# Gram products ahead of the QKV maximum pass, joined row sums in the softmax stage, and no cleared maxima, in a quantised decoder layer

## The reference

```python
def _pot_scale(x):                       # one scale for the whole tensor
    m = jnp.maximum(jnp.max(jnp.abs(x)), 1e-08)
    return jnp.exp2(jnp.ceil(jnp.log2(m / INT8_MAX)))
...
h = (x - mu) * jax.lax.rsqrt(var + LN_EPS)
h = h * fq_round(ln_gamma) + fq_round(ln_beta)
qkv = fq_floor(fq_floor(h) @ fq_round(w_qkv))
...
dots = jnp.einsum('bhnd,bhmd->bhnm', q, k) * temp
dots = fq_floor(dots)
attn = jax.nn.softmax(dots, axis=-1)
attn = fq_floor(attn)
out = jnp.einsum('bhnm,bhmd->bhnd', attn, v)
out = fq_floor(fq_floor(out) @ fq_round(w_out))
...
# cross-attention, with k and v from ctx
kv = jnp.einsum('bthd,bthe->bhde', k, v)
att = jnp.einsum('bqhd,bhde->bqhe', q, kv) * scale
```

## Time and profile before

| what | us |
|---|---|
| median of three runs | 481.63 (481.36 to 481.78) |
| the profiled execution | 479.8 |
| its span | 478.0 |
| QKV maximum pass, 28.84 to 73.34 | 44.50 |
| softmax stage, 183.73 to 317.08 | 133.35 |
| DVE busy over the span | 420.0 |
| ACT busy | 350.2 |
| PE busy | 233.2 |
| POOL busy | 149.9 |

### The profile page before, as it was taken

One profiled execution on the slowest core, in us unless ns is written; L12 is line 12 of the kernel. 1 busy time (PEld: TensorE's weight loads), 2 busy tenths in 40 slices (PEclk: granted clock), 3 DMA queues, 4 the chain that ended last, 5 costly groups with the idle time before them and its releaser, 6 DMA issues.

```text
span 478.0 us, 6808 instructions
## 1 busy us (share of the span) xinstructions
PE 233.2 (49%) x1541; PEld 106.5 (22%) x1541; DVE 420.0 (88%) x1396; ACT 350.2 (73%) x789; POOL 149.9 (31%) x323
## 2 busy tenths in 40 slices
PE   0269973878677733122222222119997718116031
PEld 0228411323122210011001111003342616102031
DVE  5879897889899999999999999958986985977967
ACT  3678983879899955999999999954776745537133
POOL 2500002001000002888889888870000005520010
PEclk9969995999755555555555555558999775557557
DMA  7500000000344520788888888792001300000002
GB/s 268 145 0 2 0 0 2 22 22 24 132 176 176 191 95 23 163 187 187 187 197 188 182 188 187 165 211 46 2 2 44 106 1 1 0 1 0 0 0 89
DMA packets 84210, 43.16 MB, mean 90 GB/s; under 512 B 69064, under 2 KB 74456, under 8 KB 84059
## 3 DMA queue, kind: packets, MB, share of 16 engines
q1 hardware_dynamic: 82618, 42.69, 34.2%
q10 hardware_dynamic: 1568, 0.21, 0.3%
HBM read 7.75 MB, written 1.58 MB: 20 GB/s over the span
## 4 chain that ended last, share of the span: by engine, by line
DVE 53%; PE 21%; issue 16%; ACT 7%; DMA 1%; DVEq 1%; ACTq 0%
PE ps L475 20%; DVE mem L1308 12%; DVE mem L1055 6%; DVE mem L1213 4%; DVE d_max L1058 4%; DVE mem L1496 2%; DVE row_max L1308 2%; DVE m L1633 2%; DVE m L1634 2%; ACT mem L903 2%; ACT mem L933 1%; DVE r_now L1054 1%; DMA bkv<-in_L_xattn_bv 1%; DVE row_code L1054 1%; DVE neg_max L1054 1%
## 5 line engine op out<-in xcount | busy, mean ns | idle before, releaser
L475 PE MATMUL ps<-mem 64*128 64x256 bf16 (+5 forms) x1188 | 175.0, 355 | 131.7 <-DMA mem<-mem 87.4
L933 ACT ACTIVATE mem<-mem,neg_max 128x256 f32<-128x256 int16 x256 | 126.2, 494 | 13.2 <-DVE neg_max L1054 9.4
L475 PEld LDWEIGHTS ps<-mem 64*128 64x128 bf16 (+3 forms) x1188 | 72.2, 122 | 229.0 <-issue 126.7
L1308 DVE CUSTOM_DVE_ANT_0 mem<-ps,fold,c 128x256 int16<-128x256 f32 x256 | 111.3, 471 | 0.0
L433 POOL TENSOR_SCALAR mem<-mem,r_now 128x256 int16<-128x256 f32 x176 | 80.9, 478 | 80.9 <-DVE r_now L1054 80.8
L1213 DVE TENSOR_TENSOR mem<-mem 128x1024 bf16<-128x1024 bf16 x82 | 54.3, 688 | 6.2 <-ACT mem L873 4.0
L888 ACT ACTIVATE mem<-ps,c 128x1024 bf16<-128x1024 f32 x48 | 48.4, 1294 | 1.6 <-PE ps L475 1.6
L933 ACT ACTIVATION_READ_ACCUMULATOR mem<-mem,neg_max 128x1 f32 x256 | 47.7, 186 | 0.0
L903 ACT ACTIVATE mem<-ps,c 128x1024 int16<-128x1024 f32 x32 | 36.4, 1211 | 13.8 <-DVEq L1250 8.5
L433 POOL TENSOR_SCALAR bv_fine<-mem,r_now 128x256 int16<-128x256 f32 x80 | 36.8, 479 | 5.0 <-DVE r_now L1054 5.0
L1058 DVE TENSOR_REDUCE d_max<-ps 128x1 f32<-128x1024 f32 (+1 forms) x34 | 38.0, 1126 | 0.3 <-PE ps L475 0.3
(11 more groups left out here) (207 smaller groups left out, 380.4 us busy)
## 6 DMA issues: line engine op xcount, KB each, us to landing
mem<-mem SPq DMA_DIRECT2D x64, 256.0 KB, 2.4
mem<-in_L_attn_w_qkv SPq DMA_DIRECT2D x1, 1536.0 KB, 9.3
mem<-in_x SPq DMA_DIRECT2D x2, 512.0 KB, 5.0
mem<-in_x SPq DMA_DIRECT2D x1, 1024.0 KB, 5.5
out<-mem SPq DMA_DIRECT2D x4, 256.0 KB, 2.2
xattn_matrix<-mem SPq DMA_DIRECT2D x1, 512.0 KB
mem<-in_L_attn_w_out SPq DMA_DIRECT2D x1, 512.0 KB, 5.0
mem<-in_L_ffn_W SPq DMA_DIRECT2D x2, 256.0 KB, 4.6
```

Source lines behind the costliest of these rows:

```text
L475: return te.matmul(o_, l_, r_, start=start, stop=stop)
L933: ins = sc.activation(e_ring[:, u % 4, pos], y_ring[:, u % 4, pos], ACT.Exp, scale=scale_reg, bias=neg_max[:, u % 4, pos:pos + 1], accum_o ...
L1308: ins = ve.tensor_tensor_reduce(y_ring[:, slot, pos], ps[:, 2 * slot + pos // 2, (pos % 2) * N:(pos % 2 + 1) * N], shift, col("g_dots"), - ...
```

## The change

- The eight Gram matrices are made in PE's queue ahead of the QKV maximum pass, four before the `across` of the weights and h and four behind it, in banks 4 to 6. ACT evicts them before and among its three w_qkv codes and at n = 1, and PE waits for two evictions before unit 2. The sums of ctx move to n = 12 and `a1` to one batch after each of n = 15 to 18 and 24 to 27. The 16 small bias activations of ACT's front are split: 8 stay, 4 come before the Gram evictions, 4 at n = 6.
- POOL's two clearings of `run_max` are gone. In both maximum passes ACT writes its first three units straight into `run_max`, and DVE starts to fold at the fourth.
- `temperature()` stands behind the semaphore that releases the first codes of the code pass.
- In the softmax stage `row_code` is float32, rounded by adding and subtracting 1.5 x 2^23. All row sums stay in `row_sums`, 128 x 256. There is one reciprocal and one `r_now` to a group, over eight rows, and no `sum_run`; one minimum over `row_sums` ends the stage. The index of `row_sums` is computed in ACT's loop for each piece. DVE's loop is written out for all 32 groups, and the order in a group is another.
- SP issues the transpose of group grp - 2 behind the copy of group grp + 4.

```diff
+WHOLE = 1.5 * 2.0 ** 23
...
-        sum_run = sb("sum_run", [P, 2, 4])
-        row_code = sb("row_code", [P, 2, 8], I16)
+        row_code = sb("row_code", [P, 2, 8])
-        row_inv = sb("row_inv", [P, 4, 4])
+        row_inv = sb("row_inv", [P, 2, 8])
-        row_sum = sb("row_sum", [P, 4, 4])
+        row_sums = sb("row_sums", [P, B * GROUPS * 8])
...
-            for grp in range(B * GROUPS - 2):
+            for grp in range(B * GROUPS):
                 if grp + STAGES < B * GROUPS:
                     stage_group("codes", grp + STAGES, grp % STAGES)
-                transpose_group(grp)
+                if grp >= 2:
+                    transpose_group(grp - 2)
...
-            pool.wait_ge(sem("gb_codes"), 1)
-            pl.memset(run_max, 0.0).then_inc(sem("run_max_zero"), 1)
-
-
-            pool.wait_ge(sem("qkv_scale"), 1)
-            pl.memset(run_max, 0.0).then_inc(sem("run_max_zero"), 1)
-
...
-            across(7, diag6[:, 2:4], 2)
-
-            def gram_half(b, part):
-                bank, pos = (6, 7, 6)[b // 3], b % 3
-                for k in range(2 * part, 2 * part + 2):
+
+            def gram_of(b):
+                bank, pos = 4 + b // 3, b % 3
+                for k in range(4):
                     last = mm(ps[:, bank, pos * (D + 1):(pos + 1) * (D + 1)], ctx_sb[:, 4 * b + k, 0:D],
                               ctx_sb[:, 4 * b + k], k == 0, k == 3)
-                if part == 1 and b in (2, 5, 7):
+                if b in (2, 5, 7):
                     last.then_inc(sem("gram_ps"), 1)
+
+            pe.wait_ge(sem("ctx_ones"), 1)
+            pe.wait_ge(sem("ctx_loaded"), 16)
+            for b in range(4):
+                gram_of(b)
+            pe.wait_ge(sem("xw_T"), 1)
+            across(7, diag6[:, 2:4], 2)
+            for b in range(4, B):
+                gram_of(b)
...
-            def a1_main(half):
-                for b in range(4 * half, 4 * half + 4):
-                    mm(ps[:, 6 + half, (b % 4) * P:(b % 4 + 1) * P], gram[:, b, 0:D], xw_T[:, 1], b % 4 == 0, False)
+            def a1_main(half, b):
+                mm(ps[:, 6 + half, b * P:(b + 1) * P], gram[:, 4 * half + b, 0:D], xw_T[:, 1], b == 0, False)
...
-                if n == 6:
-                    pe.wait_ge(sem("ctx_loaded"), 16)
-                    pe.wait_ge(sem("ctx_ones"), 1)
-                    pe.wait_ge(sem("xw_T"), 1)
                 if n == 12:
                     pe.wait_ge(sem("wh_scale"), 1)
-                if n == 18:
-                    pe.wait_ge(sem("gram_ready"), 1)
-                if 6 <= n < 22:
-                    gram_half((n - 6) // 2, n % 2)
-                if n == 27:
                     pe.wait_ge(sem("gram_ready"), 3)
-                    pe.wait_ge(sem("bias_rows"), 1)
+                    pe.wait_ge(sem("bias_rows"), 3)
                     sums_of_ctx()
-                if n == 28:
-                    a1_main(0)
-                if n == 31:
+                if n in (15, 16, 17, 18):
+                    a1_main(0, n - 15)
+                if n == 21:
                     pe.wait_ge(sem("cs_r2"), 1)
                     a1_bias(0)
-                if n == 32:
-                    a1_main(1)
-                if n == 34:
+                if n in (24, 25, 26, 27):
+                    a1_main(1, n - 24)
+                if n == 30:
                     a1_bias(1)
...
+            bias_rows(4, 6)
+            gram_eviction(0)
             act.wait_ge(sem("wh_scale"), 1)
             for k in range(3):
+                if k == 2:
+                    gram_eviction(1)
...
+                if n == 1:
+                    gram_eviction(2)
+                if n == 6:
+                    bias_rows(6, 8)
+                if n == 14:
...
-                        sc.activation(abs_t[:, nth % 3], ps[:, s:s + 2].rearrange("p a n -> p (a n)"),
+                        sc.activation(run_max[:, nth] if nth < 3 else abs_t[:, nth % 3],
+                                      ps[:, s:s + 2].rearrange("p a n -> p (a n)"),
...
-                                            accum_out=row_sum[:, u % 4, pos:pos + 1])
+                                            accum_out=row_sums[:, bass.ds(unit * 4 + pos, 1)])
...
-            temperature()
...
             dve.sem_inc(sem("cast_a"), 4)
+            temperature()
...
-            def fold_sums(grp, half):
+            def row_reciprocal(grp, half):
 
                 dve.wait_ge(sem("exp_done"), 2 * grp + 6)
-                dve.wait_ge(sem("sum_folded"), grp + 1)
-                ve.tensor_tensor(sum_run[:], sum_run[:], row_sum[:, 2 * half:2 * half + 2], ALU.min)\
-                    .then_inc(sem("sum_folded"), 1)
-
-            def row_reciprocal(unit, k):
-
-                dve.wait_ge(sem("exp_done"), unit + 5)
-                ve.reciprocal(row_inv[:, k], row_sum[:, k]).then_inc(sem("row_inv"), 1)
-
-            def row_scale(unit, k):
-
-                dve.wait_ge(sem("row_inv"), unit + 1)
-                ts(r_now[:, k], row_inv[:, k], FINE, None, ALU.mult).then_inc(sem("row_scale"), 1)
+                ve.reciprocal(row_inv[:, half], row_sums[:, 8 * grp:8 * grp + 8]).then_inc(sem("row_inv"), 1)
+
+            def row_scale(grp, half):
+
+                dve.wait_ge(sem("row_inv"), grp + 1)
+                ts(r_now[:, 2 * half:2 * half + 2].rearrange("p u h -> p (u h)"), row_inv[:, half], FINE, None,
+                   ALU.mult).then_inc(sem("row_scale"), 2)
 
             def step(grp, half, new, old):
 
-                other = 2 * (1 - half)
-                if old:
-                    row_reciprocal(2 * grp - 2, other)
                 dve.wait_ge(sem("y_ready_u"), 2 * grp + 6)
                 if new:
                     dve.wait_ge(sem("dots_codes_unit"), 2 * grp + 4 + 2 * STAGES)
-                ts(row_code[:, half], row_max[:, half], 1.0, None, ALU.mult).then_inc(sem("row_code"), 1)
+                ts(row_code[:, half], row_max[:, half], WHOLE, -WHOLE, ALU.add, ALU.add).then_inc(sem("row_code"), 1)
                 if new:
-
+                    if old:
+                        dve.wait_ge(sem("exp_done"), 2 * grp + 3)
                     codes(2 * grp + 2, 1 - half, 0, (0,))
                 dve.wait_ge(sem("row_code"), grp + 1)
                 ts(neg_max[:, 2 * half:2 * half + 2].rearrange("p u h -> p (u h)"), row_code[:, half],
                    col("ns_dots"), None, ALU.mult).then_inc(sem("neg_max"), 1)
-                if old:
-                    row_scale(2 * grp - 2, other)
                 if new:
                     codes(2 * grp + 2, 1 - half, 0, (1, 2, 3))
                 if old:
-                    row_reciprocal(2 * grp - 1, other + 1)
+                    row_reciprocal(grp - 1, 1 - half)
                 if new:
-
-                    codes(2 * grp + 3, 1 - half, 1, (0, 1))
+                    codes(2 * grp + 3, 1 - half, 1, (0,))
                 if old:
-                    row_scale(2 * grp - 1, other + 1)
-                    fold_sums(grp - 1, 1 - half)
+                    row_scale(grp - 1, 1 - half)
                 if new:
-                    codes(2 * grp + 3, 1 - half, 1, (2, 3))
+                    codes(2 * grp + 3, 1 - half, 1, (1, 2, 3))
 
             groups = B * GROUPS
-            ve.memset(sum_run[:], 3.0e38).then_inc(sem("sum_folded"), 1)
             dve.wait_ge(sem("dots_codes_unit"), 2 + 2 * STAGES)
             for k in range(2):
                 codes(k, 0, k, (0, 1, 2, 3))
             step(0, 0, True, False)
-            with dve.Fori(0, groups // 2 - 1) as i:
-                for k in range(2):
-                    step(i * 2 + 1 + k, 1 - k, True, True)
+            for grp in range(1, groups - 1):
+                step(grp, grp % 2, True, True)
             step(groups - 1, 1, False, True)
-            for k in range(2):
-                row_reciprocal(2 * groups - 2 + k, 2 + k)
-            for k in range(2):
-                row_scale(2 * groups - 2 + k, 2 + k)
-            fold_sums(groups - 1, 1)
-
-
-            dve.wait_ge(sem("sum_folded"), groups + 1)
-            link(ve.tensor_reduce(col("m"), sum_run[:].rearrange("p u h -> p (u h)"), AX.X, ALU.min))
+            row_reciprocal(groups - 1, 1)
+            row_scale(groups - 1, 1)
+
+
+            dve.wait_ge(sem("exp_done"), B * DOT_UNITS + 4)
+            link(ve.tensor_reduce(col("m"), row_sums[:], AX.X, ALU.min))
```

More of the change, by code:

```diff
@@ L821, in _, with bias_rows @@
             act.wait_ge(sem("bkv_loaded"), 32)
-            for b in range(B):
-                sc.activation(bv_sel[:, b], bkv[:, 1], ACT.Copy, scale=ident[0:B, b:b + 1])
-                ins = sc.activation(bk_sel[:, b], bkv[:, 0], ACT.Copy, scale=ident[0:B, b:b + 1])
-            ins.then_inc(sem("bias_rows"), 1)
+            def bias_rows(first, end):
+                for b in range(first, end):
+                    sc.activation(bv_sel[:, b], bkv[:, 1], ACT.Copy, scale=ident[0:B, b:b + 1])
```

(11 more changed lines are left out.)

25 lines of the change are left out of this document (12 added, 13 removed).

## The result

The changed kernel took 468.72 us (median of four runs, 468.06 to 470.23) against 481.50 (four runs, 479.68 to 481.78) before: a ratio of 0.975, 95% interval 0.971 to 0.978. The forecast was 470.1, with a range of 465 to 477. The profiled execution took 468.85 us, with a span of 467.1 against 478.0.

What follows compares the result with a forecast made beforehand. DVE was taken to bound the softmax stage, with engines waiting in turn in the QKV maximum pass. Terms -3.8 - 1.3 - 6.3 - 0.1 = -11.5 us brought the median 481.63 to 470.1, range 465 to 477.

Steps and rivals of the forecast that it cites:

- What bounds the kernel now: Softmax stage: DVE sets the 4.18 us group, ACT close behind; QKV maximum pass: no engine fills it, engines wait in turn.
- The start, -0.8: Front: without POOL's clearing the across and first units come earlier despite Gram products on PE; -0.8 us, nothing to -1.3.
- two of its signs: Front, in the new trace: the across near 23.7 us and unit 0 at 28.1 us.
- Rival 2, the clock: Front and QKV pass: the Gram move gives nothing if PE's matmuls run at half clock; 473.9 us, chance 0.12.
- The pace, -3.0: QKV maximum pass: moving Gram work out shortens eleven d_max intervals by 3.0 us, between 1.8 and 5.2.
- The first units written to `run_max`, 0: Both maximum passes: DVE's three saved folds lie behind ACT or are made up at the pass's end; zero.
- `temperature()`, -1.3: Start of the code pass: seven small DVE instructions of 0.19 us go behind the release; -1.3 us, lower bound -0.6.
- The softmax stage, -6.3: Fewer DVE instructions bring a group to 3.97 us over 32 groups; -6.3 us, bounds -7.4 and 0.
- The three floors: Softmax group: ACT needs 3.94 us, POOL 3.90, and DVE 3.94 with one wait for POOL.
- Rival 1, POOL's lock: Softmax stage: two of three small DVE operations wait for POOL, gain 0.6 instead of 6.3 us; 475.8 us, chance 0.20.
- Rival 3, the register instruction: Softmax stage: ACT's register instruction for each exponential is not hidden; 481.9 us at +0.05 a piece, chance 0.05.
- Rival 4: DVE's written-out softmax loop: new instructions sometimes come late, about 1 us in all; inside the range, no case of its own.

Runs made afterwards that it cites:

- b_nosum: The kernel before with softmax exponentials that make no row sums, so ACT's piece takes 0.40 us; its groups stay at 4.18 us.
- a_i16: The changed kernel with row_code as int16 by a multiplication with 1, as before the change; 468.73 us.
- b_nomem: The kernel before with only POOL's two clearings gone and the first three units written straight to run_max; 478.67 us (0.995).
- b_poolhalf: The kernel before, with POOL making its products over only the first 128 of each 256 columns; a softmax group takes 3.95 us.
- a_two_more: The changed kernel with two more small DVE instructions in each softmax group, behind r_now; 468.47 us.
- a_nosum: The changed kernel with softmax exponentials that make no row sums, the sums being a constant set once; its groups take 3.88 us.
- b_temp: The kernel before with only temperature() moved behind the release of the first codes; 480.24 us (0.997).
- b_gram: The kernel before with only the Gram products moved ahead, with their evictions and bias activations, POOL's clearings kept; 479.48 us (0.997).
- a_late_a1: The changed kernel with all eight remaining bias activations before the first Gram eviction, a1's second bias product and eviction behind the QKV pass's last units; 467.01 us.

## Why the prediction was right, point by point

- *What bounds the kernel now.* Right. DVE set a group's 4.18 us: with ACT's piece at 0.40 it stayed 4.18 (`b_nosum`).
- *The start, -0.8.* 0.97 in the profile, and the number is right partly by luck. The `across` came 0.74 earlier and not 1.15, as the first Gram products ran at half the pace; the forecast's 0.91 for a batch holds at the higher clock (8 records 0.11 apart), and two of its signs failed, the `across` near 23.7 and unit 0 at 28.1 (24.84 and 29.06, in both of which 0.73 is the later maximum over w_qkv). What made up for it was not in the forecast: PE, no longer idle ahead of the `across`, made it in 0.60 instead of 1.22. And ACT's first unit follows ACT's codes, not unit 0. The size does hold over more profiles: ACT's first unit is 13.29 to 14.07 behind the maximum in five with the front of before, 12.15 to 13.27 in four with the changed one, and the means are 0.88 apart. The mechanism held otherwise: the clearing had held DVE, and the Gram products then held PE.
- *Rival 2, the clock.* From 21.99 through the pass PE's granted clock was 1.00 (0.50 from 24 to 32 before); only the first seven Gram records ran at the lower pace, so it did not come. Its second half shows in one other profile: in `a_i16` the grant fell to 0.50 from 59.8 to 63.2, and the interval of `d_max` there is 3.28 instead of 2.94.
- *The pace, -3.0.* Measured from ACT's first maximum unit to the end of its last: 37.68 against 40.19, -2.5. The term that was mis-sized is what stays in the pass: I had let it cost 2.2 over eleven intervals, and the last ten alone are 2.7 over ten times 2.94. Of that 0.9 are the four bias activations, which the change itself had moved there, 1.0 the eviction of `a1` and 0.6 the interval with its second bias product.
- *The first units written to `run_max`, 0.* Right in this kernel: the folds come off DVE where it then waits for ACT (37.68 with and without them). With the Gram products still in the pass they are worth 0.43 (`b_nomem`).
- *`temperature()`, -1.3.* -1.11, and none of it came back.
- *The softmax stage, -6.3.* -7.09: a group is at ACT's own 3.93, and I had allowed 0.04 more. The three floors were sized well: 3.93 for ACT (3.94), 3.88 for POOL (3.90), 3.88 for DVE with one wait (3.94). The account of the instructions held too (0.24 forecast, 0.22 found), but it was not the only way there, and the wait was not a fixed 0.21. Before, with the wait gone and nothing removed, the group is 3.95 (`b_poolhalf`); after, with two instructions more, it is 3.93 (`a_two_more`).
- *Rival 1, POOL's lock.* Its mechanism is real and is what the stage turns on, but one small instruction waits and not two. The Trainium skill's rule ("SBUF — State Buffer", section "SBUF: two separate sides") fits in that the later one waits, but its "for the whole instruction" is not what these rows show. The operations asked for 0.06 and 0.16 us into POOL's 0.48 ended 0.02 behind its recorded end, although by themselves they last 0.23 and 0.17; so they were let go about 0.3 us into it. One asked for 0.36 in (`neg_max` at 218.29, POOL's instruction at 217.93) lasted 0.24 and did not wait. Not every small instruction is held either: the reciprocal at 222.25 before, 0.05 into POOL's instruction at 222.20, lasted 0.17.
- *Rival 3, the register instruction.* Refuted: ACT's pieces stand 0.491 apart in both kernels, with and without it.
- *Rival 4.* No gap on DVE that would tell of late instructions; `a_nosum` repeats 3.88 from group to group.

## What to carry to other kernels

Where one engine's small instructions wait for another engine, ask at what moment of the other's instruction a small one is issued: 0.2 us in a loop of 4 hung on that. An instruction added can cost nothing if it moves the small one out of the wait, and one that is reshaped in place (`row_code` as int16 or float32) changes nothing. Find the bound by making one engine artificially faster, and the next one behind it in the same run. Side work moved to another place costs its full length on an engine that has 0.1 us of room; put it where the engine idles in any case, and check that the stage behind does not give the time back.

## What was not expected of the hardware

- The clock that a window shows is only as good as its records. In `b_nomem` the column says 1.00 from 22 us on, and yet its `across` took 1.22 us and the pair of matmuls at 27.42 took 1.04, as in the earlier trace rows at 0.50. The first record of the clock in its trace stands at 31.75: the matmuls of 128x512 ahead of it last 0.58 to 0.63 each, those behind it 0.38 or 0.39. In `b_temp` the first record is at 32.47, and the pair of matmuls of a unit on either side of it reads:

```profile
29.35 1.03 PE L475 MATMUL ps<-mem 128*128 128x512 bf16 x2 [2.77 <-DVE mem L1163]
...
33.17 0.60 PE L475 MATMUL ps<-mem 128*128 128x512 bf16 x2 [0.23 <-ACT mem L873]
```

- Work given to an idle PE can speed up what follows: with the Gram products ahead of it the `across` took 0.60 (0.67 in `b_gram` and `a_i16`), and 1.22 in all six profiles without them. The clock was granted at 1.00 by then (from 21.99 in the changed kernel); before, PE had idled for 5.25 us, and it was 0.50.
- What a saving is worth can depend on when the clock is granted again: in fourteen profiles the code pass ran from 42.41 to 43.88 us in the order of that moment, and 1.1 us of `a_late_a1` went there. What sets the moment is not shown.
